# A fused GNN layer pair on one core: the second half of the main loop follows one step sooner behind the node work

## The reference

```python
edge_index = jnp.stack([src, dst])
h = jnp.maximum(_layernorm(x, axis=-1), 0.0)
# layer 0, SchNet-like: messages h[src] * filter(edge_weight), summed at dst, then an MLP
messages = (h @ W_lin.T)[senders] * (shifted_softplus(basis @ Wf1 + bf1) @ Wf2 + bf2)
agg = jax.ops.segment_sum(messages, receivers, num_segments=N_NODES)
x = x + shifted_softplus(agg @ Wm1 + bm1) @ Wm2 + bm2
h = jnp.maximum(_layernorm(x, axis=-1), 0.0)
# layer 1, SAGE-like: own part, and the mean over edges of the other end's rows
out = h @ W_self.T + b_self
neigh = h[dst] @ W_neigh.T + b_neigh
agg = jax.ops.segment_sum(neigh, src, num_segments=n)
x = x + out + agg / jnp.clip(count, 1.0, None)[:, None]
```

## Time and profile before

| | us |
|---|---|
| median of three runs | 1783.41 |
| the profiled execution's own time | 1784.23 |
| span of that execution, first to last instruction | 1780.5 |
| PE busy (matmuls) | 1571.0 (88%) |
| DVE busy | 1450.5 (81%) |
| POOL busy | 1109.2 (62%) |
| ACT busy | 1086.9 (61%) |
| mean granted TensorE clock, as a share of full | 0.949 |

### The profile page before, as it was taken

One profiled execution on the slowest core, in us unless ns is written; L12 is line 12 of the kernel. 1 busy time (PEld: TensorE's weight loads), 2 busy tenths in 40 slices (PEclk: granted clock), 3 DMA queues, 4 the chain that ended last, 5 costly groups with the idle time before them and its releaser, 6 DMA issues. The chain is left out here.

```text
span 1780.5 us, 52695 instructions
## 1 busy us (share of the span) xinstructions
PE 1571.0 (88%) x14724; PEld 1209.5 (68%) x14724; DVE 1450.5 (81%) x4720; ACT 1086.9 (61%) x2615; POOL 1109.2 (62%) x938
## 2 busy tenths in 40 slices
PE   2649868999999999999999999999999854889997
PEld 1223235777777777777777777778777754888886
DVE  8998746888888888888888888888888732788886
ACT  1007767877777777777777777777775311344443
POOL 5990054446767676676666667667674363677776
PEclk9769978999999999999999999999999975999999
DMA  3000024567777777777777777776776653999997
GB/s 86 0 0 1 9 76 129 167 204 215 218 222 220 219 216 224 216 217 227 218 210 223 220 201 200 203 204 200 197 204 187 169 154 107 261 271 279 281 282 221
DMA packets 281198, 327.49 MB, mean 184 GB/s; under 512 B 42380, under 2 KB 208782, under 8 KB 281102
## 3 DMA queue, kind: packets, MB, share of 16 engines
q1 hardware_dynamic: 204270, 248.84, 48.3%
q0 software_dynamic: 25088, 51.83, 10.3%
q10 hardware_dynamic: 51744, 25.70, 5.0%
HBM read 206.49 MB, written 119.72 MB: 183 GB/s over the span
## 5 line engine op out<-in xcount | busy, mean ns | idle before, releaser
L791 POOL DMA_INDIRECT xg<-in_x,srcs x392 | 412.8, 1053 | 379.5 <-issue 326.2
L802 POOL DMA_INDIRECT row_table<-row_out,posq x392 | 385.6, 984 | 169.5 <-issue 114.2
L1292 PE MATMUL psum<-bin_rows,bin_hot 64*128 64x129 f32 x3920 | 248.2, 279 | 46.6 <-DVE bin_hot L1264 45.6
L1292 PEld LDWEIGHTS psum<-bin_rows,bin_hot 64*128 64x128 f32 x3920 | 230.6, 190 | 64.2 <-DVE bin_hot L1264 50.5
L1134 PE MATMUL psum<-hwin,hotT 64*128 64x128 f32 x2352 | 165.1, 289 | 16.1 <-DMA hwin<-h_table 13.7
L1134 PEld LDWEIGHTS psum<-hwin,hotT 64*128 64x128 f32 x2352 | 146.9, 195 | 29.4 <-issue 16.7
L1034 ACT ACTIVATE xn<-xg,shift,rstd 128x128 f32<-128x128 f32 x392 | 161.0, 493 | 2.7 <-DVE shift L856 2.4
L1122 PE MATMUL psum<-hot,win 64*128 64x128 f32 x2352 | 159.3, 282 | 0.7 <-DVE hot L886 0.7
L1264 DVE TENSOR_TENSOR bin_hot<-iota,bin_rel 128x1280 f32<-128x1280 f32 x98 | 146.2, 1492 | 4.3
L1122 PEld LDWEIGHTS psum<-hot,win 64*128 64x128 f32 x2352 | 140.4, 189 | 12.8 <-DVE hot L886 1.1
L1100 PEld LDWEIGHTS psum<-wneigh,nhT 128*128 128x128 f32 x784 | 96.3, 192 | 70.3 <-issue 70.0
(11 more groups left out here) (174 smaller groups left out, 3667.7 us busy)
## 6 DMA issues: line engine op xcount, KB each, us to landing
win<-msg_table SPq DMA_DIRECT2D x392, 96.8 KB
hwin<-h_table SPq DMA_DIRECT2D x392, 96.0 KB
bin_rows<-row_table SPq DMA_DIRECT2D x196, 162.5 KB, 3.6
msg_table<-msgw SPq DMA_DIRECT2D x98, 258.0 KB
nx<-in_x_nodes SPq DMA_DIRECT2D x98, 256.0 KB
h_table<-h1s SPq DMA_DIRECT2D x98, 256.0 KB
y_table<-ys SPq DMA_DIRECT2D x61, 256.0 KB
out<-xg ACTq DMA_DIRECT2D x50, 256.0 KB, 3.8
```

The lines of the kernel that those rows point to most:

```text
L791: nc.gpsimd.indirect_dma_start(out=xg[:, par, t, :], out_offset=None, in_=ins["x"], in_offset=bass.IndirectOffsetOnAxis(ap=srcs[:, par, t: ...
L802: nc.gpsimd.indirect_dma_start(out=row_dram, out_offset=bass.IndirectOffsetOnAxis(ap=posq[:, par, t:t + 1], axis=0), in_=row_out[:, par, t ...
L1292: last = nc.tensor.matmul(bank[2 * slot + b][:, h * MW:(h + 1) * MW], bin_hot[half_at(b), slot % 2, w, h * P:(h + 1) * P], bin_rows[half_a ...
```

## The change

The whole row work moves from distance 13 to 18 to distance 12 to 17: `store_h1`, `load_keys`, `load_hidden`, `edge_hots`, `row_keys`, `edge_rows`, `rows_out` and `scatter` each take the quad one later in the same place of the same engine's step, and the copies of the buffers swap with it. `LAG` becomes 17, so there are 115 steps. No instruction is added or taken out of the work on a quad, and the edge and node work stay where they are.

```diff
-LAG = 18
+LAG = 17
@@ SP
-                        if there(s - 15):
-                            load_keys(s - 15, odd)
-                        if there(s - 16):
-                            load_hidden(s - 16, even)
+                        if there(s - 14):
+                            load_keys(s - 14, even)
+                        if there(s - 15):
+                            load_hidden(s - 15, odd)
                         if there(s - 3):
                             store_msg(s - 3, odd)
-                        if there(s - 13):
-                            store_h1(s - 13, odd)
+                        if there(s - 12):
+                            store_h1(s - 12, even)
@@ POOL
-                        if there(s - 18):
-                            scatter(s - 18, even)
+                        if there(s - 17):
+                            scatter(s - 17, odd)
@@ DVE
                             one_hots(s - 8, even)
-                        if there(s - 17):
-                            edge_hots(s - 17, odd)
+                        if there(s - 16):
+                            edge_hots(s - 16, even)
                         if there(s - 12):
                             hidden_out(s - 12, even)
...
-                        if there(s - 17):
-                            row_keys(s - 17, odd)
+                        if there(s - 16):
+                            row_keys(s - 16, even)
@@ ACT
-                        if there(s - 18):
-                            rows_out(s - 18, even)
+                        if there(s - 17):
+                            rows_out(s - 17, odd)
@@ PE
-                            if there(s - 18):
-                                pe.wait_ge(x_rows, s - 18 + 1)
+                            if there(s - 17):
+                                pe.wait_ge(x_rows, s - 17 + 1)
...
-                        if there(s - 17):
+                        if there(s - 16):
                             if there(s - 8):
                                 pe.wait_ge(n_aggT, s - 8 + 1)
-                            edge_rows(s - 17, odd)
+                            edge_rows(s - 16, even)
```

## The result

The changed kernel takes 1848.9 us (median of 4 runs, 1846.9 to 1857.4) against 1784.6 us for the kernel before on the same chip (1778.6 to 1790.2): ratio 1.037, 95% interval 1.034 to 1.039. It is 64 us slower where 15 us less were forecast. The profiled execution took 1846.9 us.

What follows compares the result with a forecast made beforehand. PE was taken to set the pace from 411 to 1347 us, a chain of waits the last quads. From 1784.2 us: -6.4 full steps, -1.5 clock, +1.2 filling, -2.3 node drain, -6.3 tail gave 1768.9 us, range 1761 to 1777.

Steps and rivals of the forecast that it cites:

- Same work, same places: Steps of the loop: work per quad and each piece's place in its engine's order stay the same, costed at 0.
- Filling: Pipeline start: row work starts one step sooner, so one step without it becomes a full one, +1.2 us.
- Full steps and clock: Steps 18 to 98: PE no longer waits behind DVE's h1 store waits, -6.4 us; fewer slow-clock steps, -1.5 us.
- The two slow steps: Steps 73 and 102, slow-clocked after PE waits: worth 2.9 us, perhaps chance, so 1.5 us was taken.
- the prediction's line between 1.63 and 2.0 us: PE's clock: 2.0 us of idle cost a slow step (step 73), 1.63 us in step 28 did not.
- Node drain: Steps 98 to 106: DVE's store waits in steps 100 and 101, with PE waits behind them, go: -2.3 us.
- Tail: Last quads: the last h1 store moves up one turn of SP's circle, the last scatter ends sooner, -6.3 us.
- Rival A: Message windows come last wherever the store did; only tail and filling stay: 1779.1 us, chance 0.15.
- D: Final stage's first load waits on something other than the last scatter; no tail gain: 1775.2 us, chance 0.05.
- C: SP reaches the h1 store before hidden_out is done; loads, DVE and PE wait behind: 1810 us, chance 0.02.

Runs made afterwards that it cites:

- e7: The kernel before with 2 more DVE instructions (4 already fulfilled waits) ahead of the loop of steps: 1781.9 us.
- e2: The kernel before with 4 more DVE instructions (8 already fulfilled waits) ahead of the loop of steps: 1855.4 us, ratio 1.041.
- e3: The changed kernel with 16 more DVE instructions (already fulfilled waits) ahead of its loops: 1858.0 us.
- e4: The changed kernel with 26 more DVE instructions (already fulfilled waits) ahead of its loops: 1800.2 us.
- e5: The kernel before with 48 more DVE instructions (96 already fulfilled waits) ahead of the loop of steps: 1779.3 us, ratio 0.999.
- e1: The changed kernel with 48 more DVE instructions (96 already fulfilled waits) ahead of its loops: 1770.5 us, ratio 0.993 to the kernel before.
- e8: The changed kernel with 48 more DVE instructions ahead of the loop, run once more beside e5 on one chip: 1771.0 us, ratio 0.994 to the kernel before.
- e6: The kernel before with only SP's h1 store one step sooner, DVE's program the same to the instruction: 1773.0 us, ratio 0.994.

## Why the prediction was wrong

**The step that failed** is "Same work, same places": "I cost this at 0. What hides a mistake here is little, since PE is full, so the price of a stray delay is its whole length." The second sentence came true, and more, for a delay that I had not looked for: DVE stood 61.4 us at the 12 turns, and their steps grew by 73.0. I counted instructions per quad and their order in a step, which stay the same, and not what stands in the program ahead of the loop, which grows by 4. Their own running time is nothing; what they move is the loop. By place, counted from the kernel before:

| kernel | first loop | second loop (-19) | time, us | which turns stall |
|---|---|---|---|---|
| before | 0 | -19 | 1784.6 | none |
| e7 | +2 | -17 | 1781.9 | none |
| after | +4 | -15 | 1848.9 | first loop |
| e2 | +4 | -15 | 1855.4 | first loop |
| e3 | +20 | +1 | 1858.0 | first loop |
| e4 | +30 | +11 | 1800.2 | second loop |
| e5 | +48 | +29 | 1779.3 | none |
| e1, e8 | +52 | +33 | 1770.5, 1771.0 | none |

The stall begins at +3 or +4 and has ended by +30. By the two blocks of 256 of the Trainium skill (Runtime: NRT & Kernel Launch, Instruction fetch mechanics) it would last 21 places, to +23 or +24, and every row agrees; the upper edge itself was not run. The kernel before ran 2 or 3 instructions from the edge by luck. That the place of DVE's loop decides is shown. That it is the block limit which does it is the page's account; the runs fit it, but no run changes the length of the body. The size of the blocks is open too. The packets on q14 are of 8 KB and come five to a turn, an odd number, which is hard to square with blocks of 16 KiB that are fetched whole. Were the blocks half that size, the bad places could come round twice as often, and no run stands beyond +52 to tell.

The price: the 12 stalled steps of the changed kernel add up to 214.0 us, 73.0 over 12 x 11.75. PE stood for 54.2 us in them, 4.5 in each. The rest, 1.6 us in each, is the clock: PE was busy for 13.3 us in every one of them in place of 11.75. The steps that follow (24, 28 and on to 68) lost 11.4 us at a lower clock, with no idle time in them; but in the kernel before the same steps lost 10.5 us, 9.0 of it idle, so that one loss took the place of another there. Steps 18 to 70 lost 14.8 us before and 86.7 now, so 71.8 more. In the other stretches 10.3 came back: 4.0 in steps 71 to 97, 2.4 and 6.0 in drain and tail, as forecast in kind, and 4.0 in the final stage less 6.1 ahead of step 18, which is about what these two scatter between executions.

**The other steps**, by the stretches between the same marks of PE's and SP's timeline (the openings of steps 11, 18, 98 and 107, and the first bin load). Each row stands for one profiled execution; the three without change or stall are before, e7 and e5, the two with it and no stall e1 and e8:

| us | to step 11 | 11 to 18 | 18 to 98 | 98 to 107 | 107 to first bin load | from there | span |
|---|---|---|---|---|---|---|---|
| before | 311.1 | 76.7 | 959.4 | 87.4 | 59.1 | 286.7 | 1780.5 |
| e7 | 310.0 | 75.7 | 951.9 | 90.6 | 59.1 | 289.2 | 1776.5 |
| e5 | 314.3 | 82.9 | 955.0 | 87.5 | 59.3 | 286.8 | 1785.8 |
| e1 | 312.4 | 79.5 | 952.6 | 86.1 | 52.8 | 285.2 | 1768.6 |
| e8 | 309.8 | 80.0 | 949.0 | 85.9 | 52.1 | 290.5 | 1767.3 |
| e6 | 316.4 | 75.3 | 948.9 | 85.5 | 56.4 | 290.8 | 1773.3 |
| mean of e1, e8 less mean of the three | -0.7 | +1.3 | -4.6 | -2.5 | -6.7 | +0.3 | -13.0 |
| predicted | 0 | +1.2 | -7.9 | -2.3 | -6.3 | 0 | -15.3 |

- Filling: steps 15 and 16 of e1 took 11.07 and 11.75 us where they took 10.55 and 11.06, together +1.2 as forecast. But the whole stretch scatters by 7 us between kernels that do the same (e5), so its mean confirms little.
- Full steps and clock: right in mechanism, large by 3.3 us. The execution that I worked from was the slowest of the three in these steps (959.4 against 951.9 and 955.0), so part of the store's waits that I paired (6.4 us) was that execution's. DVE's waits for the store were 9.9 us in it, 7.7 in e7 and 5.3 in e5, and PE's waits for `hidden_out` 12.6, 7.4 and 10.1; with the change and the pad these are 5.8 (e1) and 4.5 (e8), so about 5 us less where 6.4 were forecast. The two slow steps that I counted at half were of this kind: before has step 73 at 13.3 us with no wait in it, e1 has one (step 23) and e8 none. The one in e1 took 13.33 us at a granted clock of 0.90, behind a wait of PE of only 1.53 us in step 22, while 1.63 us in step 28 of the kernel before did no harm: the length of the wait alone does not decide, as the prediction's line between 1.63 and 2.0 us would have it.
- Node drain: right, -2.5.
- Tail: right. The end of the main loop in e8, which answers to the earlier trace rows:

```profile
1440.12 0.52 SPq L710 DMA_DIRECT2D h_table<-h1s  x1
...
1466.71 0.96 POOL L802 DMA_INDIRECT row_table<-row_out,posq  x1 [0.30 <-issue]
...
1476.77 2.94 SPq L1238 DMA_DIRECT2D bin_rows<-row_table  x4
```

From the last store to the end of the last scatter there are now 27.6 us (1467.7 - 1440.1), before 27.7 (1484.4 - 1456.7): the same chain of 12 scatters behind the windows, one turn of SP's circle earlier. The first bin load follows 9.1 us behind the last scatter, 9.4 before.
- Rival A falls by e6, D by the tail, and C by e8's trace: in the step from 508.95 us `hidden_out` ended at 506.86 and SP issued its store at 515.61, right behind the message store, so 8.7 us were in hand (8.8 were forecast). The chance of 0.02 for slower was too low for a reason that had nothing to do with C: I gave no chance to a cause outside the work itself.
- What the rest of the change adds to the store alone is small: e6 has 1773.0 us and e8 1771.0, and the intervals of their ratios overlap. e6 gets 2.8 us in the stretch with the tail, where I had given it none, against 6.7 for the whole change, and it has no step to fill. Whether the last 2 us are real stays open.

Of all kernels run, the changed one with the pad is the fastest, with e6, which needs no pad, level with it within the intervals.

## What to carry to other kernels

Where a tuned kernel has loops of a few hundred instructions on one engine, count that engine's instructions ahead of them, before and after an edit: an edit that leaves the body alone can still move it. In a profile the sign is idle time with releaser "issue" at the first instruction of each turn, and more packets on the instruction queue. Idle instructions ahead of the loop tell within one run, if they move it far enough: 48 did here, 16 did not (e3). Take waits from more than one execution before they are summed: 9.9 us of waits in one were 5.3 in another of the same order.

## What the runs showed of the hardware

- At a turn of its loop of 278 instructions DVE stands for 0.24 to 0.32 us in one place of the program and for 4.4 to 6.1 us in another, four instructions on, with 5 packets of 8 KB on q14. A step of 11.75 us grows to 17.1 to 18.8 by it, though DVE was busy for only 87% of the time before.
- At +20 (e3) DVE stands twice at a turn, 3.8 to 5.7 us ahead of `hot` and 1.6 to 2.9 us ahead of `hotT`, which follows it in the trace. These turns cost more: the twelve steps took 18.3 to 20.3 us.
- After idle times of 3.8 to 5.5 us PE's clock was at the lower of its two levels for a part of the same step (mean 0.86 in step 51; PE busy 13.3 us in each of the twelve) and mostly of the next (0.94); two of twelve times the next step was hardly touched (steps 32 and 44, 11.79 us each).
